# Gates of a graph network: the product of the unit sums with Wq's second half in three fp32r passes, its weights split by GpSimd inside the loop

## The reference, cut to what matters

```python
def _gate(h, q, Wg, bg, Wq, bq):
    B, L, F = q.shape                     # 8 graphs, 64 query rows, 768
    h3 = h.reshape(B, N, F)               # 32 nodes a graph
    hg = einsum('bnf,gf->bng', h3, Wg[:, :F])
    qg = einsum('blf,gf->blg', q, Wg[:, F:]) + bg
    attn = sigmoid(hg[:, :, None, :] + qg[:, None, :, :])
    qi = einsum('bnlf,blf->bnf', attn, q)
    alpha = sigmoid(einsum('bnf,gf->bng', h3, Wq[:, :F])
                    + einsum('bnf,gf->bng', qi, Wq[:, F:]) + bq)
    hn = alpha * tanh(qi) + (1.0 - alpha) * h3
```

## Time and profile before

| | us |
|---|---|
| median of 3 runs | 1119.62 |
| lowest, highest | 1117.02, 1119.64 |
| the profiled execution, its own time | 1118.25 |
| its span, first to last instruction | 1116.5 |
| TensorE busy (matmul) | 1065.0 |
| VectorE busy | 762.4 |
| ScalarE busy | 573.1 |
| GpSimd busy | 182.5 |

### The profile page before, as it was taken

One profiled execution on the slowest core, in us unless ns is written; L12 is line 12 of the kernel. 1 busy time (PEld: TensorE's weight loads), 2 busy tenths in 40 slices (PEclk: granted clock), 3 DMA queues, 4 the chain that ended last, 5 costly groups with the idle time before them and its releaser, 6 DMA issues.

```text
span 1116.5 us, 17521 instructions
## 1 busy us (share of the span) xinstructions
PE 1065.0 (95%) x7382; PEld 881.4 (79%) x7382; DVE 762.4 (68%) x1084; ACT 573.1 (51%) x604; POOL 182.5 (16%) x100
## 2 busy tenths in 40 slices
PE   6999999999999999999999989899999999999987
PEld 5889986545799964547689689758999999999974
DVE  8794755888643168885354665656888888888852
ACT  0433226888433168883243544325666666666630
POOL 3525602555100025551000000000000000000000
PEclk9999999999999999999999999999999999999999
DMA  8142285121044382220244004408777777777720
GB/s 288 13 163 92 86 273 165 58 60 55 4 170 167 123 244 59 58 58 1 85 166 171 32 1 170 166 1 296 255 254 254 243 256 244 255 243 255 245 86 29
DMA packets 82290, 163.18 MB, mean 146 GB/s; under 512 B 4044, under 2 KB 60136, under 8 KB 81918
## 3 DMA queue, kind: packets, MB, share of 16 engines
q1 hardware_dynamic: 80736, 151.86, 40.8%
q0 software_dynamic: 1472, 10.15, 3.4%
HBM read 158.35 MB, written 0.80 MB: 143 GB/s over the span
## 4 chain that ended last, share of the span: by engine, by line
PE 78%; DVE 13%; issue 4%; ACT 2%; DMA 1%; POOL 1%; SPq 0%; DVEq 0%; POOLq 0%; ACTq 0%
PE PS L1044 19%; PE PS L734 7%; PE PS L896 7%; PE PS L750 5%; PE PS L656 4%; PE PS L1027 4%; PE PS L475 4%; PE PS L1058 4%; PE PS L632 3%; PE PS L545 3%; PE PS L488 3%; PE PS L557 3%; PE PS L790 2%; PE PS L961 2%; DVE PRD L1630 1%
## 5 line engine op out<-in xcount | busy, mean ns | idle before, releaser
L1864 DVE TENSOR_TENSOR Wlo<-W,Whi 128x2304 fp32r<-128x2304 f32 x68 | 173.7, 2555 | 43.5 <-ACT Whi L1383 43.5
L1383 ACT CAST Whi<-W 128x2304 fp32r<-128x2304 f32 x68 | 144.5, 2127 | 0.0
L1044 PE MATMUL PS<-Whi,Mhi 128*128 128x384 f32 x408 | 137.9, 338 | 0.0
L1044 PE MATMUL PS<-Wlo,Mhi 128*128 128x384 f32 x408 | 136.5, 334 | 0.0
L1044 PE MATMUL PS<-Whi,Mlo 128*128 128x384 f32 x408 | 136.4, 334 | 0.0
L447 POOL TENSOR_TENSOR PRDP<-arena 128x1024 f32<-128x1024 f32 x48 | 114.6, 2387 | 113.1 <-PE PS L750 84.2
L734 PE MATMUL PS<-QH,SEL 128*128 128x512 f32 x384 | 115.8, 422 | 5.1 <-ACT xT L1223 1.4
L1244 ACT ACTIVATE arena<-PS 128x1024 f32<-128x1024 f32 x96 | 98.5, 1026 | 23.4 <-PE PS L734 23.4
L734 PEld LDWEIGHTS PS<-QH,SEL 128*128 128x128 f32 x384 | 64.8, 188 | 55.0 <-DVE PRD L1630 21.2
L1244 ACT ACTIVATE PS<-PS 128x1024 f32<-128x1024 f32 x96 | 98.0, 1021 | 2.6 <-PE PS L734 2.6
L1044 PEld LDWEIGHTS PS<-Whi,Mlo 128*128 128x128 f32 x408 | 76.7, 188 | 0.0
(11 more groups left out here) (288 smaller groups left out, 2367.5 us busy)
## 6 DMA issues: line engine op xcount, KB each, us to landing
W<-in_L_rel SPq DMA_DIRECT2D x68, 1152.0 KB, 5.6
W<-in_W_rel SPq DMA_DIRECT2D x6, 2304.0 KB, 8.7
W<-in_W SPq DMA_DIRECT2D x6, 2304.0 KB, 8.4
arena<-in_qU SPq DMA_DIRECT2D x96, 128.0 KB, 2.6
W<-in_WqT SPq DMA_DIRECT2D x4, 2304.0 KB, 9.7
W<-in_W_root SPq DMA_DIRECT2D x2, 2304.0 KB, 13.8
W<-in_WgT SPq DMA_DIRECT2D x2, 2304.0 KB, 9.1
QH<-QH POOLq DMA_DIRECT2D x2, 1536.0 KB, 9.9
```

What stands on the lines that cost most here:

```text
L1044: mm = pe.matmul(PS[:, 4 + s % 2, 0:HALF], MS[a][mb][:, k, j * P:(j + 1) * P], WS[b][w % 3][:, k, :], start=n == 0, stop=n == 17)
L1383: nc.scalar.copy(WS[0][w % 3][:], W[(FIRST34 + r) % 2][:, :, q * HALF:(q + 1) * HALF]).then_inc(w_hi, 1)
L1864: V.tensor_tensor(WS[1][w % 3][:], W[(FIRST34 + r) % 2][:, :, q * HALF:(q + 1) * HALF], WS[0][w % 3][:].bitcast(F32), ALU.subtract).then_i ...
```

## The change

The product at line 790 becomes three fp32r passes. The sums are split by ScalarE (`sums_high`, a cast) and VectorE (a subtraction in place of the copy), into `QIS`. Wq's second half is split by GpSimd in the loop: behind each of its products number 2 to 19 (counted from 0) of a gate stands one `split_piece`, 512 columns wide, by turns a cast into `WH` and a subtraction in place into `WR` (the same memory as `W`). TensorE waits for all 18 pieces of a gate ahead of the product. Since `WH` is used until the second gate, the five bias rows are loaded when gate 1's product is done (`w_used` 15), and VectorE waits for them at their first use. The split of the second third of `W_root2` goes behind the gate parts. Two waits with semaphores of their own are made with the step counters; they stand on no path that is spoken of here.

```diff
             for w in range(9, 12):
                 third_lo_first(w)
-            pool.wait_ge(wr_used, 3 * (R3 + 1))
-            for i, n in enumerate(("b_gcn", "L1_b", "L2_b1", "L2_b2", "b_rgcn")):
-                pool.dma_start(biasN[:, i, :], A[n].partition_broadcast(P)).then_inc(small_in, 16)
+            def split_piece(g, n):
+
+                m = 7 * g + 7
+                if n == 0:
+                    pool.wait_ge(w_in[m % 2], 16 * (m // 2 + 1))
+                q, ks = n // 6, slice(2 * (n // 2 % 3), 2 * (n // 2 % 3) + 2)
+                whole, high = third_turned(W[m % 2], q)[:, ks], WH[q][:, ks]
+                if n % 2 == 0:
+                    nc.gpsimd.tensor_copy(high, whole).then_inc(wq_split, 1)
+                else:
+                    pool.wait_ge(wq_split, 18 * g + n)
+                    nc.gpsimd.tensor_tensor(third_turned(WR[m % 2], q)[:, ks], whole, high.bitcast(F32), ALU.subtract
+                                            ).then_inc(wq_split, 1)
...
                     nc.gpsimd.tensor_tensor(PRDP[k % 2], SIGP, QD[h], ALU.mult).then_inc(pool_prod, 1)
-
+                    if 2 <= k < 20:
+                        split_piece(g, k - 2)
+
+            pool.wait_ge(w_used, 15)
+            for i, n in enumerate(("b_gcn", "L1_b", "L2_b1", "L2_b2", "b_rgcn")):
+                pool.dma_start(biasN[:, i, :], A[n].partition_broadcast(P)).then_inc(small_in, 16)
...
                 weights(m0 + 6)
-                Wq2 = W[(m0 + 6) % 2]
+                pe.wait_ge(wq_split, 18 * (g + 1))
 
                 def alpha_part(m, ks):
 
+                    Wq2 = (WH[m // 2], third_turned(WR[(m0 + 6) % 2], m // 2))
                     for k in ks:
-                        mm = pe.matmul(PS[:, m // 2, (m % 2) * NODES:(m % 2 + 1) * NODES], Wq2[:, k, m * P:(m + 1) * P], qiT[:, k, :],
-                                       start=k == 0 and m % 2 == 0, stop=k == KC - 1 and m % 2 == 1, skip_group_check=True)
+                        for a, b in ((0, 0), (1, 0), (0, 1)):
+                            mm = pe.matmul(PS[:, m // 2, (m % 2) * NODES:(m % 2 + 1) * NODES], Wq2[b][:, k, m % 2, :],
+                                           QIS[a][k // 2][:, k % 2, :], start=k == 0 and a == b == 0 and m % 2 == 0,
+                                           stop=k == KC - 1 and b == 1 and m % 2 == 1, skip_group_check=True)
...
+                def sums_high(j):
+
+                    act.wait_ge(qi_turned, 3 * g + j + 1)
+                    nc.scalar.copy(QIS[0][j][:], PS[:, 4 + j, :].rearrange("p (k n) -> p k n", k=2)).then_inc(qi_hi, 1)
+
+                sums_high(0)
+                sums_high(1)
                 for j in range(3):
+                    if j == 2:
+                        sums_high(2)
...
                 if g == 0:
                     third_hi_turned(0)
-                    third_hi_turned(1)
...
+                if g == 0:
+                    third_hi_turned(1)
...
-                    dve.wait_ge(qi_turned, 3 * g + j + 1)
-                    V.tensor_copy(qiT[:, 2 * j:2 * j + 2, :], PS[:, 4 + j, :].rearrange("p (k n) -> p k n", k=2)).then_inc(qiT_copied, 1)
+                    dve.wait_ge(qi_hi, 3 * g + j + 1)
+                    V.tensor_tensor(QIS[1][j][:], PS[:, 4 + j, :].rearrange("p (k n) -> p k n", k=2), QIS[0][j][:].bitcast(F32),
+                                    ALU.subtract).then_inc(qiT_copied, 1)
...
                 if g == 0:
                     third_lo_turned(0)
-                    third_lo_turned(1)
...
+                if g == 0:
+                    third_lo_turned(1)
...
+                if n == 1:
+                    dve.wait_ge(small_in, SMALL)
...
-            dve.wait_ge(small_in, SMALL)
```

More of the change, by code:

```diff
@@ L87 @@
 EHALF = EC // 2
+ROWS2_SET = 4
 def build(nc, A):
@@ L155, in build @@
         QD = [view(arena, 12032 + 1024 * i, 1024) for i in range(2)]
-        qiT, tanhT = put("qiT", [P, KC, NODES], F32, 100)[:], MT[0][:]
+        tanhT = MT[0][:]
+        QIS = [[put(f"QI{x}{j}", [P, 2, NODES], F32R, at + 2 * j) for j in range(3)] for x, at in (("hi", 100), ("lo", 84))]
         alphaT = hqT = xT[:]
@@ L246, in build @@
         pool_step, consts = sem("pool_step"), sem("consts")
-        rows2_set, bg_hi, bg_ready, half_read = sem("rows2_set"), sem("bg_hi"), sem("bg_ready"), sem("half_read")
+        bg_hi, bg_ready, half_read = sem("bg_hi"), sem("bg_ready"), sem("half_read")
         dve_step = sem("dve_step")
@@ L260, in build @@
         pool_prod = sem("pool_prod")
+        wq_split, qi_hi = sem("wq_split"), sem("qi_hi")
         qi_copied, qi_turned, qiT_copied, tanh_done = sem("qi_copied"), sem("qi_turned"), sem("qiT_copied"), sem("tanh_done")
@@ L269, in build @@
         gcn_scaled, gcn_sum = sem("gcn_scaled"), sem("gcn_sum")
-        cn_turned, cn_copied, cn_ready = sem("cn_turned"), sem("cn_copied"), sem("cn_ready")
+        cn_turned, cn_copied = sem("cn_turned"), sem("cn_copied")
         rows_done, xT_dve, hT_act, hT_dve, evicted = (sem(n) for n in ("rows_done", "xT_dve", "hT_act", "hT_dve", "evicted"))
@@ L384, in _ @@
             then(nc.gpsimd.memset(ROWS2F[0:1, :], 1.0))
-            nc.gpsimd.memset(ROWS2F[32:33, :], 1.0).then_inc(rows2_set, 1)
-            pool.wait_ge(rows2_set, 1)
+            then(nc.gpsimd.memset(ROWS2F[32:33, :], 1.0))
+            rows2_set = steps[0]
+            assert rows2_set == ROWS2_SET
             then(nc.gpsimd.iota(relid[:], pattern=[[1, R34]], base=0, channel_multiplier=0,
@@ L1154, in third_hi_first @@
                 nc.scalar.copy(WH[(w + 1) % 3][:], third_turned(W[m % 2], w % 3)).then_inc(wr_hi, 1)
-            act.wait_ge(rows2_set, 1)
+            act.wait_ge(pool_step, ROWS2_SET)
             nc.scalar.copy(ROWS2[:], ROWS2F[:]).then_inc(bg_hi, 1)
@@ L1748, in _ @@
             dve.wait_ge(cn_copied, 1)
-            V.tensor_scalar(NM, CN, 0.5, MASKED, ALU.is_lt, ALU.mult).then_inc(cn_ready, 1)
-            dve.wait_ge(cn_ready, 1)
+            then(V.tensor_scalar(NM, CN, 0.5, MASKED, ALU.is_lt, ALU.mult))
             u0 = 0
```

## The result

The changed kernel takes 1123.94 us (median of 5 runs, 1123.56 to 1125.98), the kernel before 1118.06 (5 runs, 1116.87 to 1119.64): ratio 1.0053, 95% interval 1.0039 to 1.0067. It is slower by 5.9 us, as forecast in sign, near the forecast's 1125 and inside its range. The profiled execution took 1124.02, with a span of 1122.3; clock 0.993 (before 0.995).

The account below looks back on a forecast made before the run. TensorE looks full, but a longer path through ScalarE, GpSimd's product and VectorE's operations was taken to bound the loop. 1118.25 - 4.8 (start and tails) + 11.7 (loop) = 1125 us; own range 1121 to 1129, 8 in 10 1113.5 to 1133.

Parts of the forecast that it names:

- Start: Ahead of gate 0: without the bias broadcasts beside it, Wq's first half loads in time and TensorE's wait goes, -1.3 us.
- Tail of gate 0: Behind gate 0's loop: earlier gate parts, less what the moved W_root2 split takes back, -1.4 us.
- Tail of gate 1: Behind gate 1's loop: 28 products as three fp32r passes, each 0.075 us shorter, all on the path, -2.1 us.
- Loop: Both gates' loops: split pieces and VectorE's two-SBUF-input operations delay each other, 0.65 us a pair, 18 pairs, +11.7 us.
- the operations above 2 us: Expected sign in the new profile: VectorE's two-input operations in the loop exceed 2 us in some turns.
- The +0.3: In the loop: a subtraction that goes second overruns its gap and pushes the next GpSimd product, about +0.3 us.
- the subtractions go behind the products of that kind: In the loop: subtractions follow the odd products, where VectorE's operation is issued within 0.1 us of the product's end.
- VectorE's op always goes first: +2 to +5: Lower bound of the loop: 8.82 to 9.0 us per eight steps against 8.73, so +2 to +5 us.
- order kept: Rival for the loop: VectorE is always first, loop +2 to +5, total say 1117 us; chance 0.22.
- Hidden: Rival for the loop: the pieces cost nothing in GpSimd's idle time, total 1113.5 us; chance 0.15.
- Pieces first: Rival for the loop: queued pieces go ahead of VectorE's operation, loop +15 to +23, total 1129 to 1137; chance 0.15.
- No gain in the tails: Rival for the tails: passes no faster or gate parts gave nothing, tails give only -1.3, total 1128.5; chance 0.06.

Follow-up runs that it names:

- kernel with the fp32 product: Kernel before with the bias loads moved and the second third of W_root2 split behind the gate parts, Wq's product still fp32: 1116.62 us, 0.9981.
- constants: Changed kernel with each piece replaced by a GpSimd write of constants that reads nothing, weights not split: 1114.06 us, 0.9978.
- casts alone: Changed kernel with the 18 subtractions left out, low passes taking the high parts: 1115.04 us, 0.9976.
- the wait for VectorE: Changed kernel with each piece waiting until VectorE's two-input product of that turn is done: 1121.08 us, 1.0034.
- a third ahead: Changed kernel with a third of Wq's second half split ahead of the loop, the rest in 18 pieces waiting behind VectorE's two-input product: 1115.55 us, 0.9972.
- subtractions alone: Changed kernel with the 18 casts left out, so the high parts are stale: 1124.93 us, 1.006.
- a third ahead without the wait: Changed kernel with a third split ahead and smaller pieces in the loop, each starting when the GpSimd product ends: 1115.93 us, 0.9974.

## Why the prediction was right

**Start, -1.3.** Measured -1.26, and -1.68 where the loads alone are moved. The wait of 1.33 is gone in each. The agreement to 0.04 is luck: in the ten other kernels with the moved loads the first product starts at 180.29 to 181.47, or 0.9 to 2.0 earlier than before. The new place costs nothing on the path, by the cover that was named: 14.73 of its 18.02 us are left.

**Tail of gate 0, -1.4.** Measured -1.32, step by step at the times worked out (302.40, 307.73, 310.17). The kernel with the fp32 product shows that three quarters of it are the moved third of `W_root2`, not the passes. Five other kernels with this tail have -0.3 to -0.4 only, by the clock (last section), which was no term of the sum.

**Tail of gate 1, -2.1.** Measured -1.99, where the kernel with the fp32 product has none of it (506.47 to 539.19, 32.72). That the cast and the subtraction ahead of it give back what the first 8 products save holds too: the third pair of blocks waits 1.40 (0.78 before for the copy), and goes on 8.40 after the loop's last product, where it was 8.36 (517.83 - 509.47).

**Loop, +11.7.** The mechanism was right: VectorE's two-input operation and a reading GpSimd instruction keep each other out for the whole instruction, with the operations above 2 us that the forecast named as its sign, and subtractions go by turns second and first (233.56, 242.22). The term was mis-sized. It is +9.6, by pair 0.53 and not 0.65: one pair of the turn costs 1.12 (forecast +1.0), the other 0.00 (forecast +0.3). The +0.3 was the subtraction that goes second and pushes the next product; it does push the one at 235.79, but the next comes 4.08 later, and both steps together take 8.67.

**One reason inside the loop term was wrong, one bound stays unmeasured.** The step "the subtractions go behind the products of that kind" made the order hang on which product a piece follows; with the pieces shifted by one product the loss is the same, +10.4. The lower bound, "VectorE's op always goes first: +2 to +5", was not measured by itself: the run that forces this order has +7.0, a pair of 9.10 where the budget said 8.82 to 9.0, but 0.4 of that pair is the run's own wait. What the rival "order kept" would have cost stays open.

**The rivals.** Hidden falls (1114.55 without the pieces, 1123.94 with them). Order kept falls, as eight operations were held by a subtraction that went first. Pieces first (by its own sum 1128.5 to 1136.5) falls: of the four two-input operations of a turn one is stretched by a whole subtraction, the others take 1.23 to 1.57. No gain in the tails falls by the two lines above. A loss of 0.8 in the encoder stage was in no case; it comes from TensorE's clock.

The forecast's 1125.0 against 1124.02 of the profiled execution is then -2.1 in the loop term, +0.2 in the three gains and +0.8 in the rest. That the total is within 1 us, closer than its largest term, is luck: the clock's 0.8 had no part in the sum.

## What to carry to other kernels

An idle engine isn't a free one: the idle share of GpSimd said nothing of what its pieces did to VectorE. Ask for each piece which instruction on the critical path needs what the piece holds, and which of the two comes first: here a piece of 1.28 behind VectorE's operation cost nothing and one ahead of it 1.12 a turn. A sum of the shared resource alone doesn't tell it; 8.5 in a period of 8.73 still cost all of the loss. What helped was both together: smaller pieces behind VectorE's operation, and a third of the split done ahead of the loop, turned +0.5% into -0.3%. And try each part of a compound change alone, since the two that only moved work gave 2.1 us.

## What was not expected of the hardware

GpSimd's recorded duration of an instruction holds its wait for the port: the same cast has 0.60 and 1.62, the same subtraction 1.28 and 2.27, with no idle time shown. Prices are to be read from the minimum of a line, and a median far above it is the sign of the wait.

When a piece was queued behind a product, VectorE's operation went ahead of it if it was already issued (233.33, ahead of 233.56), and behind it if it was issued 0.12 later than the piece's start (242.34, after 242.22). With the pieces shifted by one product 0.01 was enough (228.50, after 228.49; it took 2.35).

In these runs TensorE's clock took back small gains in places far away. Besides the stretches above, five of the kernels that keep the changed tail (no pieces, constants, casts alone, the wait for VectorE, a third ahead) have their middle at 126.7 and not 125.75, with the clock down in gate 0's tail, here without pieces:

```profile
304.00:312.00 8.00, 6.13 (x39) 5.93 (x38) 6.60 (x8) 3.46 (x3) 0.00 (x0) 0.79 0.61 247
```

In the changed kernel the same stretch has 1.00, behind the same waits of 0.84 and 1.87, and so it is in three others (subtractions alone, shifted, a third ahead without the wait). What decides between the two was not settled. The difference of the middles is 1.0 us, and the version that beat both kernels is among the five that pay it.
